# Sixteen expert blocks of the first ten tiles run while the last tiles are routed; weights split in 58 steps

## The chip, the cores and the metric
One core of one Trainium2 chip runs the whole program. The engines of the core are TensorE (PE), VectorE (DVE), ScalarE (ACT), GpSimd (POOL) and SyncE (SP), which mostly issues DMAs. The metric is the device time of one execution in microseconds; the median of the runs is compared.

## The reference
The input `x` is 2048 tokens (16 tiles of 128) of width 512. Four sublayers follow each other, each with a layer norm and a residual:
```
x = x + xattn0(layernorm(x), ctx, seg_id)       # 16 heads, keys masked to a window of 9 by seg_id
x = x + moe(layernorm(x))                       # 16 experts of width 352, 6 per token
x = x + xattn1(layernorm(x), ctx, mask)         # one head, 128 memory tokens
x = x + (mlp + product-key experts)(layernorm(x))
# moe:
scores = softmax(h @ gate_w.T); topk_w, topk_idx = top_k(scores, 6)
y = sum over e of cw[:, e] * ((silu(h @ w_gate[e].T) * (h @ w_up[e].T)) @ w_down[e].T)
```
All products are float32 in the reference; the kernel takes most of them as three float16 products (high times high, high times low, low times high).

## The kernel before, in words
The stretch of the program that matters runs from the first attention to the end of the mixture of experts.

**Attention (to about 576 us).** The loop runs over 64 steps (`STEPS`), four heads of one tile of 128 tokens in each. PE's step is `scores(m)`, the queries of the next tile (`heads_pe`, `rope_pe`), `turn_prob(m-2)`, `values(m-3)`, `outputs(m-4)`; ACT and DVE between them make exponentials, maxima and the high and low halves. When a tile's four steps are through, DVE adds its output to `x` (`add_outputs`) and the tile goes to routing some steps later: `token_rows` and `logits` on PE, softmax, the best six, a mask and a rank on DVE (`route_scores` ... `route_rank`). Tiles are routed in batches: two at a time, the last four one at a time. POOL's `place` writes, for each tile and each of its six choices, 128 token numbers of 4 bytes to the places in `expert_tokens` that the ranks give (96 indirect DMAs in all). ACT stores each tile's normalized row with its gate weights to `token_rows` (`row_store`) and `x` to `x_sum` (`x_store`).

**The split.** Beside it, `split_act` and `split_dve` turn the expert weights, in 128 pieces, into a high and a low half in `expert_w`: SP loads a piece into one of four stage buffers, ACT makes the high half (L1361), DVE the low one (L1578), SP stores both. Every step takes two pieces, so the split fills all 64 steps.

**The table.** When the last tile is ranked, PE counts tokens per expert (L1051 and before), DVE works out which block of 128 tokens belongs to which expert (L2005 to L2028) and writes a row of numbers (`tabrow`, L2031). Blocks are numbered 0 to 110 (`NBLK` = 111). SP waits for that row, for all stores to `token_rows` and for all places (L758 to L764), then loads the lists of the first blocks (`records`, L712 and L714) and the weights that are still missing.

**Experts (about 616 to 1300 us).** For block b POOL gathers 128 rows (`gather_rows`, L2298), PE turns them (`turn_rows`, L1061), does gate and up (`expert_up`, 24 matmuls), turns the hidden layer (`turn_hidden`, L1088) and does down (`expert_down`, 9 matmuls); ACT copies, takes silu and scales the result (`rows_out`), DVE multiplies and copies, POOL adds the result to `x_sum` by an indirect DMA with accumulation (L2311). Only one such add is in flight at a time. The blocks go in the order of the experts; four weight slots (`SLOTS`) are filled ahead, and `expert_loads` and `down_loads` refill a slot when its expert's last block is through. The weights of one expert are 1408 KB (`wa`) and 768 KB (`wd`).

After the last block the program reads `x_sum` back and goes on with the second attention and the MLP.

Each engine executes its own instructions in the order in which the program writes them; nothing reorders them. What decides is therefore where a call stands in an engine's list and which semaphore it waits for.

## Time and profile before
| | us |
|---|---|
| median of 3 runs | 1932.38 |
| lowest, highest | 1922.26, 1932.46 |
| the profiled execution | 1926.74 |
| its span | 1925.0 |
| TensorE busy in the span | 1801.6 |
| VectorE, ScalarE, GpSimd busy | 1093.7, 884.7, 820.2 |

The mean granted TensorE clock is 0.977 of full speed. Matmuls overlap, so a busy PE is one that always has a matmul under way. The stretches below are in microseconds from the start of the span: the head until about 96, attention until about 576, the experts from 616 to about 1300, the rest after that.

### The profile page before, as it was taken

The numbers are of one execution on the slowest core, as the hardware profiler recorded it, in microseconds if no ns is written. First come the engines' busy times: TensorE is split into PE (matmuls) and PEld (weight loads), VectorE is DVE, ScalarE is ACT, GpSimd is POOL, SyncE is SP. The second block draws the span as 40 slices with busy tenths as digits, with TensorE's granted clock in tenths as the row PEclk, the third lists the DMA queues.
The fourth block names the chain that finished last, engine by engine and source line by source line (L and its number), as shares of the span: only waits on it lengthen the run. The fifth ranks groups of instructions, "written<-read, shape, count | busy, mean of one in ns | idle before, by whom it ended". The sixth has DMA issues, their size and how long they took to land.

```text
span 1925.0 us, 39526 instructions
## 1 busy us (share of the span) xinstructions
PE 1801.6 (94%) x12786; PEld 1073.8 (56%) x12789; DVE 1093.7 (57%) x2985; ACT 884.7 (46%) x1833; POOL 820.2 (43%) x731
## 2 busy tenths in 40 slices
PE   6989999999972999999999999995899999999998
PEld 3566666766631666666666666663554444444444
DVE  4578888888852323322322323223656877777776
ACT  4588888888841443444434434433732221122111
POOL 4234456656664344443433443442112444544442
PEclk9999999999985999999999999998999999999999
DMA  8255587777776666766665765545012355555653
GB/s 310 88 163 175 178 164 168 186 178 170 182 161 166 159 147 145 160 163 152 146 150 135 165 153 100 93 82 129 33 35 66 125 187 202 206 171 210 203 178 143
DMA packets 137921, 294.81 MB, mean 153 GB/s; under 512 B 39200, under 2 KB 64416, under 8 KB 133600
## 3 DMA queue, kind: packets, MB, share of 16 engines
q1 hardware_dynamic: 86752, 157.47, 29.5%
q0 software_dynamic: 46368, 126.29, 26.7%
q10 hardware_dynamic: 4608, 8.52, 1.5%
q8 instruction: 115, 1.88, 0.4%
q14 instruction: 78, 0.64, 0.1%
HBM read 426.00 MB, written 78.33 MB: 262 GB/s over the span
## 4 chain that ended last, share of the span: by engine, by line
PE 81%; DVE 6%; DMA 4%; issue 4%; ACT 3%; POOL 1%; SPq 0%; another core or an unknown queue 0%; ACTq 0%; POOLq 0%; DVEq 0%
PE bank L234 21%; PE bank L236 21%; PE bank L235 21%; PE bank L1061 3%; PE bank L1088 2%; PE bank L851 1%; DVE work_arena L1578 1%; DMA x_sum<-x,work_arena 1%; PE bank L927 1%; ACT xt_arena L1314 1%; PE bank L842 1%; POOL expert_tokens L2226 1%; DMA work_arena<-in_ctxT 1%; DMA work_arena<-in_pk_w 1%; DMA work_arena<-in_moe_w 1%
## 5 line engine op out<-in xcount | busy, mean ns | idle before, releaser
L234 PE MATMUL bank<-work_arena,xt_arena 128*128 x1221 | 404.7, 331 | 2.8 <-DVE xt_arena L2072 1.9
L235 PE MATMUL bank<-work_arena,xt_arena 128*128 x1221 | 404.6, 331 | 0.0
L236 PE MATMUL bank<-work_arena,xt_arena 128*128 x1221 | 404.5, 331 | 0.0
L2311 POOL DMA_INDIRECT x_sum<-x,work_arena x111 | 176.5, 1590 | 392.5 <-DMA x_sum<-x,work_arena 222.9
L2060 DVE TENSOR_TENSOR xt_arena<-xt_arena,bank 128x352 f32<-128x352 f32 x111 | 57.9, 522 | 405.9 <-PE bank L236 373.0
L234 PE MATMUL bank<-work_arena 128*128 128x512 f16 (+1 forms) x600 | 226.3, 378 | 15.1 <-DVE x L1883 6.8
L235 PE MATMUL bank<-work_arena 128*128 128x512 f16 (+1 forms) x600 | 226.4, 379 | 0.0
L236 PE MATMUL bank<-work_arena 128*128 128x512 f16 (+1 forms) x600 | 226.3, 378 | 0.0
L1468 ACT ACTIVATE xt_arena<-bank 128x1024 f16<-128x1024 f16 x111 | 113.6, 1023 | 224.4 <-PE bank L1061 212.0
L234 PE MATMUL bank<-xt_arena,work_arena 128*128 128x512 f16 x528 | 200.1, 379 | 1.7 <-DVE xt_arena L194 1.7
L235 PE MATMUL bank<-xt_arena,work_arena 128*128 128x512 f16 x528 | 200.1, 379 | 0.0
L236 PE MATMUL bank<-xt_arena,work_arena 128*128 128x512 f16 x528 | 200.1, 379 | 0.0
L2318 POOL TENSOR_TENSOR work_arena<-work_arena 128x512 f16<-128x512 f32 x64 | 73.3, 1164 | 267.7 <-ACT work_arena L1453 267.7
L236 PEld LDWEIGHTS bank<-work_arena,xt_arena 128*128 128x128 f16 x1221 | 119.7, 98 | 85.1
L234 PEld LDWEIGHTS bank<-work_arena,xt_arena 128*128 128x128 f16 x1221 | 119.8, 98 | 82.6 <-issue 3.3
L235 PEld LDWEIGHTS bank<-work_arena,xt_arena 128*128 128x128 f16 x1221 | 119.7, 98 | 79.4
L2327 POOL DMA_INDIRECT work_arena<-in_pk_e,work_arena x128 | 135.0, 1055 | 36.7 <-issue 33.4
L2298 POOL DMA_INDIRECT x<-token_rows,work_arena x111 | 112.0, 1009 | 49.7 <-issue 27.7
L1578 DVE SCALAR_TENSOR_TENSOR work_arena<-work_arena 128x704 f16<-128x704 f32 (+2 forms) x90 | 89.9, 1001 | 70.8 <-ACT work_arena L1361 54.1
L2212 POOL TENSOR_TENSOR xt_arena<-xt_arena,work_arena 128x512 f32<-128x512 f32 x64 | 66.8, 1043 | 137.0 <-DVE work_arena L1668 133.9
L1314 ACT ACTIVATE xt_arena<-xt_arena,work_arena 128x128 f32<-128x128 f32 x256 | 123.2, 482 | 2.1
L1487 ACT ACTIVATE x<-bank,xt_arena 128x512 f32<-128x512 f32 x111 | 76.3, 687 | 99.6 <-PE bank L236 92.6
(278 smaller groups left out, 3823.0 us busy)
## 6 DMA issues: line engine op xcount, KB each, us to landing
work_arena<-expert_w SPq DMA_DIRECT2D x111, 1408.0 KB
work_arena<-expert_w SPq DMA_DIRECT2D x111, 768.0 KB
work_arena<-in_moe_w SPq DMA_DIRECT2D x64, 352.0 KB
expert_w<-work_arena SPq DMA_DIRECT2D x64, 352.0 KB
work_arena<-in_moe_w SPq DMA_DIRECT2D x64, 192.0 KB
expert_w<-xt_arena SPq DMA_DIRECT2D x64, 192.0 KB
work_arena<-in_mlp_w SPq DMA_DIRECT2D x8, 1536.0 KB
work_arena<-in_head_w SPq DMA_DIRECT2D x16, 512.0 KB, 5.6
```

The source lines that it names most:

```text
L234: pe.matmul(o, a_hi, b_hi, start=start, stop=False)
L235: pe.matmul(o, a_hi, b_lo, start=False, stop=False)
L236: return pe.matmul(o, a_lo, b_hi, start=False, stop=stop)
L1314: last = act.activation(prob[:, m % 3, i, :], prob[:, m % 3, i, :], ACT.Exp, bias=ebias[:, m % 4, i:i + 1], scale=seg_scale[:, t:t + 1], a ...
L1468: act.activation(xT[:, b % 2, :], bank[4][:, :].bitcast(F16), ACT.Copy).then_inc(xt_cp, 1)
L1487: act.activation(ysb[:, b % YB, :], bank[6 + b % 2][:, :], ACT.Copy, scale=ecw[:, b % 4, :]).then_inc(y_cp, 1)
L1578: return dve.scalar_tensor_tensor(out=o, in0=src, scalar=scale, in1=hi, op0=ALU.mult, op1=ALU.subtract)
L2212: pool.tensor_tensor(prob[:, m % 3, :, :], prob[:, m % 3, :, :], rinv[:, m % 4, :].unsqueeze(2).to_broadcast([P, 4, P]), ALU.mult).then_in ...
L2298: pool.indirect_dma_start(out=xbu[:, b % XB, :], out_offset=None, in_=rows[:, :], in_offset=bass.IndirectOffsetOnAxis(ap=rid[:, i:i + 1], ...
L2311: pool.indirect_dma_start(out=xacc[:, :], out_offset=bass.IndirectOffsetOnAxis(ap=rid[:, i:i + 1], axis=0), in_=ysb[:, b % YB, :], in_offs ...
L2318: pool.tensor_tensor(h_lo[:, S_ % 2, c, :], m2[:, c, :], h_hi[:, S_ % 2, c, :], ALU.subtract).then_inc(hlo, 1)
L2327: pool.indirect_dma_start(out=gbuf[:, n % 2 * SETS + i - FIRST[n], :], out_offset=None, in_=ins["pk_e"][:, :], in_offset=bass.IndirectOffs ...
```

## The change
A first part of the expert work is taken out of the tokens that are routed early. After ten tiles (`EARLY_TILES`) the tokens per expert are counted. Only whole blocks of 128 tokens of one expert count; the first 16 of them (`EARLY`) in the order of the experts become blocks 0 to 15, and the table for them is made on DVE in steps 61 and 62 (`early_blocks`, `early_columns`) and written after step 63 (`early_row`). SP takes the first four experts' numbers out of that table, and waits for the stores and places of the first ten tiles only. The other blocks follow as 16 to 110, with a table made while the early blocks run; the experts of the early blocks come up a second time in them, so that their weights are loaded twice. The last steps of routing move into the expert loop: tiles 14 and 15 (now one batch) are turned, ranked and counted between the matmuls of blocks 0 to 8, and 24 places move from before the first gather to behind it. `outputs(STEPS - 1)`, the last product of attention, comes after the first `turn_rows`. Banks are shared with the tail of attention, so that blocks below 13 (`EARLY_Y`) write their result to one bank instead of two. The attention arrays lie in another order in `work_arena`, and the tables lie elsewhere; the gate and up weights of three experts are loaded there before attention is over. The split of the 128 pieces is spread over the first 58 steps: 46 of them take two pieces and 12 take three, the last six take none.

The diff, cut to its core:
```diff
+SPLIT_STEPS = 58
+EARLY_TILES, EARLY = 10, 16
+EARLY_Y = 13
+assert (EARLY_TILES * P * TOPE - E * (P - 1)) // P >= EARLY
...
         att_a_lo = wr.take(H, 2 * P, dt=F16)
-        att_vo_hi = wr.take(H, D, dt=F16)
-        att_vo_lo = wr.take(H, D, dt=F16)
-        att_vo_end = wr.at
         PW, SW = DC * 384, 256 + 2048
...
+        att_vo_hi = wr.take(H, D, dt=F16)
+        att_vo_lo = wr.take(H, D, dt=F16)
+        att_vo_end = wr.at
...
-        BATCHES = [(a, 2) for a in range(0, NT - 4, 2)] + [(a, 1) for a in range(NT - 4, NT)]
-        INNER = len(BATCHES) - 2
+        BATCHES = [(a, 2) for a in range(0, NT - 4, 2)] + [(NT - 4, 1), (NT - 3, 1), (NT - 2, 2)]
+        INNER = len(BATCHES) - 1
...
+        EARLY_Q = next(q for q, (a, _) in enumerate(BATCHES) if a == EARLY_TILES)
+        COUNT_AT = ready(EARLY_Q) + 2
...
-            return [(i, i % NPC) for i in (2 * m, 2 * m + 1) if 0 <= i < E * NPC]
+            return [(i, i % NPC) for i in range(E * NPC) if i * SPLIT_STEPS // (E * NPC) == m]
...
+        def y_bank(b):
+            return bank[6] if b < EARLY_Y else bank[6 + b % 2]
...
+            def first_expert(r):
+                return sp.value_load(tabrow[0:1, FIRST_RUNS + r:FIRST_RUNS + r + 1], min_val=0, max_val=E - 1)
+            def first_a(r, e):
+                sp.dma_start(wa[:, r * 2 * AW:(r + 1) * 2 * AW],
+                             wsp[ds(e, 1), :, 0:2 * AW].rearrange("a p n -> p (a n)")).then_inc(load_a[r], 16)
+            def first_d(r, e):
+                at = (r + 1) % SLOTS * 2 * DW
+                sp.dma_start(wd[:, at:at + 2 * DW],
...
-            sp.wait_ge(routed, TABLE_ROW)
+            sp.wait_ge(q_free, q_at["early_cols",] + 1)
             sp.wait_ge(padded, 32)
-            sp.wait_ge(xacc_in, 16 * (NT + 1))
+            sp.wait_ge(xacc_early, 16 * (EARLY_TILES + 1))
             for s in range(SLOT_ROWS):
-                sp.wait_ge(row_out[s], 16 * len(range(s, NT, SLOT_ROWS)))
-            sp.wait_ge(placed, 16 * TOPE * NT)
-            sp.dma_start(rid[:, 0:1], recs[0:P, :]).then_inc(first_list, 16)
+                sp.wait_ge(row_out[s], 16 * len(range(s, EARLY_TILES, SLOT_ROWS)))
+            sp.wait_ge(placed_early, 16 * TOPE * EARLY_TILES)
+            firsts = [first_expert(r) for r in range(SLOTS)]
+            for s in range(STAGES):
+                sp.wait_ge(split_out[s], 16 * len(range(s, E * NPC, STAGES)))
+            sp.wait_ge(q_mm, q_at["heads", NT - 1, 3] + 1)
+            first_a(0, firsts[0])
             records(0)
-            records(1)
-            first_a(2)
-            first_d(3)
-            first_a(3)
+            first_a(1, firsts[1])
+            first_a(2, firsts[2])
+            sp.wait_ge(rope_h, 2 * NT)
+            sp.wait_ge(rope_l, 2 * NT)
+            sp.dma_start(rc2, ins["route_c2"]).then_inc(route_in, 16)
+            for n in range(1, EARLY // REC_BATCH):
+                records(n)
+            sp.wait_ge(y_mm, STEPS)
+            first_d(0, firsts[0])
+            first_a(3, firsts[3])
+            for r in range(1, SLOTS):
+                first_d(r, firsts[r])
             held = {}
             for b in range(NBLK + 5):
-                if b % REC_BATCH == 0 and 1 < b // REC_BATCH + 2 < (NBLK + REC_BATCH - 1) // REC_BATCH:
+                if b == MAIN_AT:
+                    sp.wait_ge(routed, TABLE_ROW)
+                    sp.wait_ge(xacc_in, 16 * (NT - EARLY_TILES))
+                    for s in range(SLOT_ROWS):
+                        sp.wait_ge(row_out[s], 16 * len(range(s, NT, SLOT_ROWS)))
...
+                if m == COUNT_AT:
+                    pe.wait_ge(masked, EARLY_Q + 1)
+                    q_room_free(pe, "early_count")
+                    pe.matmul(q_bank("early_count")[:, 0:E], one16, seen16, start=True, stop=True).then_inc(q_mm, 1)
...
+            pe.wait_ge(routed, EARLY_SET)
+            q_room_free(pe, "early_cols")
+            for i in range(4):
+                last = pe.matmul(q_bank("early_cols")[0:1, i * P:(i + 1) * P], tcol16[:, i:i + 1], id16[:, :],
+                                 start=True, stop=True)
...
+                if b == 0:
+                    pe.wait_ge(smax, STEPS)
+                if b == 1:
+                    pe.wait_ge(yadd, NT)
+                o = bank[1 if b == 0 else 4][:, :].bitcast(F16)
...
+                if 0 < b < EARLY_Y:
+                    pe.wait_ge(y_cp, b)
+                elif b >= EARLY_Y:
...
+            pe.wait_ge(q_free, q_at["early_cols",] + 1)
             slots = {b: slot_of(b) for b in range(2)}
             turn_rows(0)
+            outputs(STEPS - 1)
+            expert_up(0, slots[0])
             turn_rows(1)
-            expert_up(0, slots[0])
             for b in range(NBLK - 3):
                 expert_up(b + 1, slots[b + 1])
+                if b == 0:
+                    token_rows(14)
+                if b == 1:
+                    logits(14)
+                if b == EARLY_Y + 1:
+                    pe.wait_ge(routed, TABLE_ROW)
                 slots[b + 2] = slot_of(b + 2)
                 turn_rows(b + 2)
                 turn_hidden(b)
                 if b > 0:
                     expert_down(b - 1, slots.pop(b - 1))
+                if b == 1:
+                    pe.wait_ge(q_free, q_at["logits", 14] + 1)
+                    token_rows(15)
+                if b == 2:
+                    logits(15)
+                if b == 4:
+                    ranks(LASTQ)
+                if b == 5:
+                    route_count()
+                if b == 7:
+                    route_cols()
...
-            rows_turned(14)
             x_store(14)
             row_store(13)
             values_high(STEPS - 1)
-            gate_exps(Q14)
-            row_store(14)
-            row_high(15)
-            rows_turned(15)
-            x_store(15)
-            gate_exps(Q15)
-            row_store(15)
...
             rows_copy(0)
+            x_store(15)
+            row_high(15)
+            expert_silu(0)
             rows_copy(1)
-            expert_silu(0)
             hidden_high(0)
...
                 expert_silu(b + 1)
+                if b in (0, 2):
+                    rows_turned(14 + b // 2)
                 if b + 2 < NBLK:
                     rows_copy(b + 2)
                 hidden_high(b + 1)
+                if b == 2:
+                    gate_exps(LASTQ)
+                if b == 4:
+                    row_store(14)
+                    row_store(15)
             rows_out(NBLK - 2)
...
+            def early_blocks():
+                dve.wait_ge(rope_l, 2 * NT)
+                dve.wait_ge(q_free, q_at["early_count",] + 1)
+                dve.memset(run_up, 0.0)
+                dve.memset(early_sum, 0.0)
+                dve.memset(early_used, 0.0)
+                then(dve.tensor_tensor(tcmp, early_cnt.unsqueeze(2).to_broadcast([P, E, 15]),
+                                       rc_step.unsqueeze(1).to_broadcast([P, E, 15]), ALU.is_ge))
+                then(dve.tensor_reduce(early_full, tcmp, AX.X, ALU.add))
+                running_sum(early_end, early_full)
+                then(dve.tensor_scalar(early_sum[:, 1:E + 1], early_end, float(EARLY), None, ALU.min))
+                then(dve.tensor_tensor(early_used[:, 0:E], early_sum[:, 1:E + 1], early_sum[:, 0:E], ALU.subtract))
+                then(dve.tensor_scalar(early_is, early_used[:, 0:E], 0.0, None, ALU.is_gt))
+                running_sum(early_run, early_is)
...
+                if m == STEPS - 3:
+                    early_blocks()
+                if m == STEPS - 2:
+                    early_columns()
...
+            early_row()
...
+            add_outputs(15)
+            row_stats(15)
+            for s in range(STAGES):
+                dve.wait_ge(split_out[s], 16 * len(range(s, E * NPC, STAGES)))
+            dve.wait_ge(route_in, 16 * 8)
+            choose(0, EARLY, early_end, rc_blk[:, 0:EARLY])
+            row_normalize(15)
+            expert_weight(0)
             hidden(0)
             hidden_low(0)
             for b in range(NBLK):
-                expert_weight(b)
+                if b > 0:
+                    expert_weight(b)
                 if b == NBLK - 2:
                     hidden_copy(b)
                 if b + 1 < NBLK:
                     hidden(b + 1)
+                if b == 1:
+                    keep_logits(14)
                 if b != NBLK - 2:
                     hidden_copy(b)
                 if b + 1 < NBLK:
                     hidden_low(b + 1)
+                if b == 2:
+                    keep_logits(15)
+                    route_scores(LASTQ)
+                if b == 3:
+                    route_softmax(LASTQ)
+                    route_best(LASTQ)
+                    route_mask(LASTQ)
+                if b == 4:
+                    route_rank(LASTQ)
+                if b == 5:
+                    main_blocks()
+                    main_columns()
+                if b == 7:
+                    main_row()
+                if b == 8:
+                    choose(EARLY, NBLK, tend, rc_blk[:, 0:NBLK - EARLY])
                 if b in (20, 21, 23):
                     memory_masks((20, 21, 23).index(b))
...
-                if m in (STEPS - 2, STEPS - 1):
-                    place_batch(INNER - 2, 3 * (m - STEPS + 2), 3 * (m - STEPS + 3))
-            normalize(STEPS - 1)
-            row_rstd(14)
-            row_low(14)
-            place_batch(INNER - 1, 0, TOPE)
-            place_batch(Q14, 0, 1)
-            row_rstd(15)
-            row_low(15)
-            place_batch(Q14, 1, TOPE)
-            place_batch(Q15, 0, TOPE)
...
+            normalize(STEPS - 1)
+            row_rstd(14)
+            row_low(14)
+            gather_rows(0)
+            gather_rows(1)
+            gather_rows(2)
+            gather_rows(3)
+            row_rstd(15)
+            row_low(15)
+            gather_rows(4)
+            gather_rows(5)
+            gather_rows(6)
             for b in range(NBLK):
-                if b + ROWS_AHEAD < NBLK:
+                if b < 4:
+                    place_batch(INNER - 2 + b // 2, 3 * (b % 2), 3 * (b % 2) + 3)
+                elif b < 7:
+                    place_batch(LASTQ, 4 * (b - 4), 4 * (b - 3))
+                if ROWS_AHEAD + 2 <= b + ROWS_AHEAD < NBLK:
                     gather_rows(b + ROWS_AHEAD)
                 pool.wait_ge(y_cp, b + 1)
                 if b > 0:
```

On GpSimd's list the end of attention and the start of the experts read as follows before. `expert_tokens` is what `place` writes, `x<-token_rows` is a gather of rows, `x_sum<-x` the add of a block's result.
```order
L2222 TENSOR_TENSOR xt_arena<-xt_arena 128x512
L2226 DMA expert_tokens<-work_arena 38784x1 x3
L2212 TENSOR_TENSOR xt_arena<-xt_arena,work_arena 128x512
L2226 DMA expert_tokens<-work_arena 38784x1 x6
...
L2222 TENSOR_TENSOR xt_arena<-xt_arena 128x512
L2226 DMA expert_tokens<-work_arena 38784x1 x7
L2218 TENSOR_TENSOR ln_rs<-ln_ve,neg_half 128x1
L2222 TENSOR_TENSOR xt_arena<-xt_arena 128x512
L2226 DMA expert_tokens<-work_arena 38784x1 x11
L2298 DMA x<-token_rows,work_arena 128x528 x6
```
And now:
```order
L2416 TENSOR_TENSOR xt_arena<-xt_arena 128x512
L2476 DMA x<-token_rows,xt_arena 128x528 x4
L2412 TENSOR_TENSOR ln_rs<-ln_ve,neg_half 128x1
L2416 TENSOR_TENSOR xt_arena<-xt_arena 128x512
L2476 DMA x<-token_rows,xt_arena 128x528 x3
L2420 DMA expert_tokens<-work_arena 38784x1 x3
L2503 DMA x_sum<-x,xt_arena 2176x512
L2420 DMA expert_tokens<-work_arena 38784x1 x3
L2503 DMA x_sum<-x,xt_arena 2176x512
L2420 DMA expert_tokens<-work_arena 38784x1 x3
```
Seven gathers have moved ahead of the places of tiles 12 to 15, and those places stand between the adds of blocks 0 to 6, three or four at a time.

On SP's list the loads of the first experts before (`expert_w` 128x5632 is an expert's gate and up, 128x3072 its down, `expert_tokens` one block's list):
```order
L689 DMA work_arena<-in_route_c 128x367
L692 DMA work_arena<-expert_w 128x5632
L696 DMA work_arena<-expert_w 128x3072 x3
L692 DMA work_arena<-expert_w 128x5632
L765 DMA work_arena<-expert_tokens 128x1
L712 TENSOR_LOAD work_arena
```
And now, with a load of a number from the table (`TENSOR_LOAD`) ahead of each:
```order
L721 TENSOR_LOAD xt_arena
L721 ISA x2
L724 ISA
L724 DMA work_arena<-expert_w 128x5632
L739 TENSOR_LOAD xt_arena
L739 ISA x2
L741 ISA
L741 DMA xt_arena<-expert_tokens 128x1
...
L724 DMA work_arena<-expert_w 128x5632
L724 ISA
L724 DMA work_arena<-expert_w 128x5632
L803 DMA work_arena<-in_route_c 128x367
```
The first weight load now stands behind four numbers out of the table; the down weights come after twelve more lists and after the end of attention.

## Rows read from the trace of the kernel before

**Rows 1.** Page, forty slices: TensorE clock granted, in tenths.
```profile
PEclk9999999999985999999999999998999999999999
```

**Rows 2.** Windows: busy us by engine, PEclk, DMA share, GB/s.
```profile
96.00:480.00 384.00, 369.80 (x3825) 259.58 (x3824) 318.13 (x1027) 322.91 (x839) 206.38 (x183) 1.00 0.70 173
...
540.00:560.00 20.00, 13.83 (x89) 7.44 (x87) 11.08 (x43) 10.99 (x31) 16.02 (x16) 0.84 0.64 160
...
560.00:580.00 20.00, 13.60 (x80) 6.39 (x78) 9.39 (x36) 4.04 (x7) 8.61 (x9) 0.84 0.82 167
...
580.00:600.00 20.00, 2.45 (x27) 1.62 (x27) 6.79 (x37) 1.31 (x3) 11.91 (x12) 0.50 0.98 184
...
600.00:620.00 20.00, 5.21 (x28) 3.43 (x29) 3.48 (x5) 3.33 (x3) 6.44 (x5) 0.50 0.35 84
...
624.00:626.00 2.00, 2.00 (x18) 1.35 (x16) 0.38 (x3) 0.46 (x1) 0.00 (x0) 1.00 1.06 437
...
700.00:1300.00 600.00, 600.00 (x4480) 381.92 (x4479) 181.86 (x480) 243.07 (x380) 247.59 (x191) 1.00 0.63 136
```

**Rows 3.** Chain that ended last, 594 to 616: start, us, what.
```profile
594.89 11.17 DMA expert_tokens<-work_arena
...
610.12 1.97 DMA work_arena<-expert_tokens
...
612.35 3.15 DMA x<-token_rows,work_arena
```

**Rows 4.** Timeline of PE, 573 to 632: start, us, instruction.
```profile
573.38 0.38 PE L235 MATMUL bank<-work_arena 128*128 128x512 f16 x1
...
573.59 0.38 PE L236 MATMUL bank<-work_arena 128*128 128x512 f16 x1
...
615.82 1.01 PE L1061 MATMUL bank<-id,x 128*128 128x128 f16 x8 [1.21 <-DMA x<-token_rows,work_arena]
...
625.82 0.61 PE L1061 MATMUL bank<-id,x 128*128 128x128 f16 x8
...
631.22 0.61 PE L1061 MATMUL bank<-id,x 128*128 128x128 f16 x8
```

**Rows 5.** Timeline of SP's queue, 576 to 616.
```profile
576.27 0.34 SPq L692 DMA_DIRECT2D work_arena<-expert_w  x1
...
607.54 7.50 SPq L714 DMA_DIRECT2D work_arena<-expert_tokens  x7
```

**Rows 6.** Timeline of POOL, 562 to 643.
```profile
562.75 1.16 POOL L2222 TENSOR_TENSOR xt_arena<-xt_arena 128x512 f16<-128x512 f32 x1 [3.21 <-ACT xt_arena L1333]
...
593.62 0.97 POOL L2226 DMA_INDIRECT expert_tokens<-work_arena  x1 [0.30 <-issue]
...
635.11 1.63 POOL L2311 DMA_INDIRECT x_sum<-x,work_arena  x1 [14.16 <-ACT x L1487]
...
641.41 1.59 POOL L2311 DMA_INDIRECT x_sum<-x,work_arena  x1 [3.38 <-ACT x L1487]
```

**Rows 7.** Timeline of DVE, 547 to 592.
```profile
547.02 0.89 DVE L1578 SCALAR_TENSOR_TENSOR work_arena<-work_arena 128x704 f16<-128x704 f32 x1 [3.13 <-ACT work_arena L1361]
...
553.89 0.24 DVE L1714 TENSOR_TENSOR work_arena<-work_arena 128x16 f32<-128x16 f32 x1
...
588.06 0.41 DVE L2005 TENSOR_TENSOR work_arena<-bank,work_arena 128x240 f32<-128x240 f32 x1 [0.29 <-issue]
...
591.93 0.16 DVE L2028 SCALAR_TENSOR_TENSOR work_arena<-work_arena 128x1 f16<-128x1 f32 x1
```

**Rows 8.** Groups by form, 96 to 480: busy, mean ns, idle before.
```profile
L1361 ACT ACTIVATE work_arena<-work_arena 128x704 f16<-128x704 f32 x53 | 41.1, 775 | 0.9 <-DMA work_arena<-in_moe_w 0.9
...
L1361 ACT ACTIVATE xt_arena<-work_arena 128x384 f16<-128x384 f32 x53 | 27.0, 509 | 0.9 <-DMA work_arena<-in_moe_w 0.9
...
L1578 DVE SCALAR_TENSOR_TENSOR work_arena<-work_arena 128x704 f16<-128x704 f32 x53 | 47.3, 892 | 56.8 <-ACT work_arena L1361 43.5 <-issue 12.8
...
L1578 DVE SCALAR_TENSOR_TENSOR xt_arena<-work_arena,xt_arena 128x384 f16<-128x384 f32 x53 | 48.1, 907 | 0.0
```

307 lines of the change are left out of this document (179 added, 128 removed).

## The prediction
> **What bounds the kernel now.** I read the page's clock line first. The granted TensorE clock is full everywhere except in three of the forty slices of 48.1 us, the 12th and 13th (529 to 626 us) and the 28th (from 1299) [rows 1]. Then the windows. From 700 to 1300 PE is busy 600.00 of 600 us, from 96 to 480 it is 369.80 of 384: both long stages are bound by PE, with ACT at 322.91 and DVE at 318.13 of 384 close behind in attention [rows 2]. Between them lies the hole. From 540 to 620 PE is busy 13.83, 13.60, 2.45 and 5.21 of 20 us each, so 44.9 of 80 us are idle, and from 580 to 600 the granted clock is 0.50, the lower of the two levels (1.2 GHz) [rows 2].
>
> Then the chain of waits, to see what fills the hole. The last attention matmul starts at 573.59 [rows 4], SP sees its count at 576.27 [rows 5], and the first `turn_rows` that leads into `expert_up(0)` starts at 615.82 [rows 4]. In between stand the ranking of tiles 14 and 15, their places at 1.27 us each (0.97 busy and 0.30 issue) [rows 6], a landing of the last place of 11.17 us, the first list in 1.97 and the first gather in 3.15 us [rows 3]. None of it is PE's work. The change lets PE begin before it.
>
> **Where the blocks start afterwards.** I follow the new chain in the times of the old trace.
> DVE can write the early table when `route_scores` of step 63 is through, 553.89 + 0.24 [rows 7], since the two split pieces behind it are gone. Four small copies at about 0.2: 555.0.
> SP then loads four numbers, issues the first weights and loads four lists. Seven pairs of a number and a list take 7.50 us, 1.07 each [rows 5]; a DMA issue alone takes 0.34 of that [rows 5], a number 0.73. So 4 × 0.73 + 0.34 + 4 × 1.07 = 7.5: 562.5. The last list lands 1.97 later [rows 3]: 564.5.
> POOL is free by then: its `row_low(14)` stands at 562.75 [rows 6], and places that stood ahead of it are gone. Gather 0 lands after 3.15 [rows 3]: 567.7. It shares the DMA engines with 2.8 MB of weights that SP issues at 562.5; at 437 GB/s [rows 2] they take 6.6 us. Bounds: 567.7 if the gather slips between them, 574.3 if it comes behind all. I take 571, the middle, since there is no row of a gather under such load.
> PE gets there earlier: matmuls of 512 columns follow each other at 0.21 us (573.38, 573.59 [rows 4]), so an `outputs` of 12 takes 2.6, and `outputs(62)` ends that much before 573.97, at about 571.3; the split pieces gone from the last DVE and ACT lists give about 2 back. So PE waits 1 or 2 us for the gather, and `turn_rows(0)` is at 571.
> Then, at full clock: turn 0.5, `outputs(63)` 2.6, `expert_up(0)` 3.5 (24 matmuls of 352 columns, 24 × 0.21 × 352/512): 577.6. `turn_rows(1)` has its copy on ACT behind `row_high(15)` and `expert_silu(0)`, which wait for DVE's norm of tile 15: I put 3 us there. `expert_up(1)` 3.5, `token_rows(14)` 0.5: `turn_rows(2)` stands at 585.1, where it stands at 625.82 now [rows 4]. `turn_rows(3)`, with 1.6 for ACT's added copy, comes at 591.3 against 631.22 [rows 4]. The shift is 40 us. It includes the 3.5 us that `expert_up(0)` costs more now, at the lower clock of [rows 2].
>
> **What has to be paid back, term by term.**
> PE's small work for routing (two `token_rows`, two `logits`, rank, two tables) moves from an idle to a busy PE: about 1.5 us.
> POOL in blocks 2 to 6: three or four places at 1.27, a gather, taken like a place, at 1.27, and an add at 1.59 + 0.3 [rows 6] are 7.0 to 8.3 us, where one block takes 6.30 (641.41 − 635.11 [rows 6]). The lag is 2 × 0.7 + 3 × 2.0 = 7.4 us. Gathers are issued five blocks ahead and PE is up to two behind POOL, some 6 to 12 us of cover; so between 0 and 7. The places' own landing (11.17 once [rows 3]) can delay a gather behind them. I take 3, the bounds are 0 and 11.
> DVE's table work: 19 instructions from 588.06 to 592.09 [rows 7], 0.21 each. `main_blocks` and `main_columns` are 23, 4.9 us, in a block where DVE is busy 181.86/600 × 6.3 = 1.9 of 6.3 us [rows 2]: an overrun of 0.5, and PE needs that result only a block later. Nothing; without that cover 0.5.
> `early_blocks` and `early_columns` are 18 and 30 instructions, 3.8 and 6.4 us, in steps 61 and 62. There DVE waits now, 3.13 us at 547.02 for the split piece alone [rows 7], and two pieces (1.8 us) a step are gone. Net about 1 us later; the bounds are −3 (the pieces were the limit) and +6 (all of it on the path).
> The split over 58 steps: 12 steps with a third piece. ACT pays (41.1 + 27.0)/106 = 0.64 a piece, DVE (47.3 + 48.1)/106 = 0.90 [rows 8]. A step lasts 384/54 = 7.1 us (54 steps fit into these 384 us), ACT is busy 6.0 of it and DVE 5.9 [rows 2]; with a third piece 6.6 and 6.8. Still below 7.1, so PE sets the time: 1 us in all, with 0 and 12 × 0.9 = 11 as bounds.
> Weights: five experts (ten tiles give 480 tokens per expert on average, so mostly three whole blocks each) are loaded twice, 11 MB more, in a stage whose DMA share is 0.63 [rows 2]. The first four experts, 8.9 MB, must be in by block 3; at 437 GB/s that is 20 us, from 558 to 600 there are 42. Nothing; 0 to 5. One bank for the results: `expert_down(b)` waits for a copy that ACT does a whole `expert_up` earlier, nothing. The arena's order changes addresses only.
>
> Sum: 40 − 1.5 − 3 − 1 − 1 = 33.5 us. The profiled execution took 1926.74, which gives 1893. That is 5.6 below the median of the three runs and 4.5 above the lowest, so it stands for a middling run; I predict 1893.5.
>
> **A rule beside the rows.** The last place, 128 numbers of 4 bytes, took 11.17 us to land [rows 3]. The Trainium skill ("DMA: Bandwidth & Descriptors", section "Anatomy of one DMA — SWDGE (gpsimd) path") has about 2.0 us fixed plus the bytes at 436 GB/s for a DMA that GpSimd issues. For the place that is an estimate of 2 us, five times under the row; for a gather of 264 KB 2.6, and the row has 3.15 [rows 3]. By the page the POOL term would be 0 and the sum 36.5; I stay with 3, because the places here came in a dense series beside weight loads, and in the new order gathers stand among them. The same page ("Specifications") says that pieces under 512 bytes cost a read-modify-write, which speaks against putting 4-byte writes into the busy stage; the row does not separate that from queueing.
>
> **The rivals.**
> (a) The queue of small writes. Places, gathers and adds share POOL and one DMA queue; blocks 3 to 12 wait for their rows, because a gather stands behind four places and each add must have landed before the next. For it: the 11.17 us [rows 3] and 8.3 against 6.3 us. Against: the cover of two blocks. Price 10 to 15 more than my 3: about 1905. Chance 0.17.
> (b) Slower. The ring of four stage buffers sets the pace of attention: then the 58 steps take as long as the 64 do, the last six come on top with 6 × 7.1 = 43 us, and the 10.2 us of early tables are on the path too. 33.5 − 43 − 8 gives 17 slower, 1944. It decides from the point where a piece takes over 7.1/2.2 = 3.2 us round trip per stage. Against it: ACT waited only 0.9 us for 53 loads of each size [rows 8], and PE is busy 96% [rows 2]. Chance 0.04.
> (c) No gain: blocks start early, but PE stands at block 14 or before it for the second table, lists or weights until about the old time. SP's wait for the table needs DVE's last copy in block 7, two blocks before SP gets there; a slip of four blocks (25 us) leaves 8 us, 1919 to 1925. Chance 0.05.
> (d) Better. The last steps of attention, where PE is busy only 69% from 540 to 560 [rows 2], shrink by 6 us or so, and the places cost nothing: about 1884. Chance 0.16.
> My forecast, 1887 to 1900: 0.58.
>
> **How the numbers follow.** Half a percent, 9.7 us, is about what the runs can tell from no change. Faster by more: the forecast, (a), (d) and a part of (c), 0.91. Within: most of (c), 0.05. Slower: (b), 0.04. The range 1879 to 1912 takes in nearly all of (d) and of (a), with 1 to 2 in 10 left out.
>
> **What would show it.** In the new trace the first `turn_rows` starts near 571 and not after 575; the windows from 580 to 620 have PE busy at least 17 of 20 us and the clock at 1.00; `turn_rows(2)` is near 585. POOL's adds of blocks 2 to 6 are over 6.3 us apart and PE idles up to 3 us for rows around blocks 9 to 12; if it idles 10 or more, (a) holds. Attention's last matmuls before the table come at 551 ± 4; if at 590, (b). The end of the experts comes 30 to 37 us earlier than now. If attention is later by more than 10 us, or the blocks start after 590, the prediction is wrong.

## The result: slower by 1.3%

| | median of the runs | range |
|---|---|---|
| before | 1930.49 us | 1922.26 to 1932.46 |
| after | 1955.46 us | 1942.31 to 1961.43 |

The ratio is 1.0132, with 1.0079 to 1.0186 as its 95% interval. Measured once more beside other kernels it was 1.0100 [1.0072, 1.0127]. I had forecast 1893.5 us, a range of 1879 to 1912, and "slower" with 0.04. The prediction was wrong in sign.

The profiled execution of the changed kernel took 1942.31 us (span 1940.5), against 1926.74 (1925.0) before, 15.6 us more. It is the fastest of the four runs behind the second median, so the profiles account for 15.5 of the 25 us between the medians. The first sign is on the page: where [rows 1] have two low slices at the border of attention and experts, this line has three shallow ones.

```profile
PEclk9999999999998889999999999998999999999999
```

The windows, in the columns of [rows 2]:

```profile
96.00:480.00 384.00, 363.30 (x3739) 256.07 (x3737) 321.42 (x1015) 318.67 (x825) 207.79 (x177) 0.98 0.73 186
...
560.00:580.00 20.00, 15.78 (x91) 7.27 (x87) 12.59 (x60) 6.67 (x18) 5.82 (x6) 0.99 0.48 153
580.00:600.00 20.00, 10.46 (x63) 6.21 (x64) 4.38 (x12) 4.70 (x6) 7.30 (x8) 0.75 0.65 235
600.00:620.00 20.00, 15.69 (x135) 10.54 (x133) 3.82 (x12) 6.73 (x10) 6.07 (x6) 0.91 0.95 308
620.00:640.00 20.00, 19.12 (x154) 11.97 (x151) 7.30 (x31) 9.90 (x14) 12.59 (x12) 1.00 0.62 88
640.00:660.00 20.00, 15.15 (x95) 8.41 (x95) 8.81 (x43) 5.01 (x8) 7.58 (x8) 0.91 0.61 141
660.00:680.00 20.00, 14.58 (x93) 8.68 (x94) 4.73 (x12) 4.43 (x7) 14.48 (x13) 0.83 0.65 57
680.00:700.00 20.00, 12.14 (x76) 6.99 (x73) 5.92 (x15) 5.22 (x9) 6.46 (x5) 0.83 0.76 142
700.00:1300.00 600.00, 595.38 (x4420) 378.03 (x4421) 179.25 (x474) 240.66 (x377) 245.40 (x188) 0.99 0.66 154
```

The hole of [rows 2], with PE at 2.45 of 20 us, is filled in part: PE does 10.46 and 15.69 from 580 to 620. But from 640 to 700 it has only 41.87 of 60 us, at 0.83 to 0.91 of the clock. The DMA engines move 57 to 142 GB/s there at a busy share of 0.61 to 0.76. That pair alone says little: [rows 2] have 0.63 at 136 in the steady stage, where PE is full. The steady stage afterwards is as before, 595.38 of 600. What was won before 620 is lost again before 700, and more.

I followed two markers through each trace: the last maxima of an attention step (DVE), and the output of a block (ACT, `rows_out`), which comes every 6.3 us when nothing is in the way.

| marker, us | before | after | shift |
|---|---|---|---|
| maxima of step 24 | 268.2 | 276.0 | +7.8 |
| maxima of step 56 | 496.3 | 509.5 | +13.2 |
| maxima of step 63 | 547.9 | 563.0 | +15.1 |
| first `turn_rows` | 613.58 | 586.66 | −26.9 |
| output of block 0 | 634.1 | 615.8 | −18.3 |
| output of block 16 | 735.0 | 751.3 | +16.3 |
| end (span) | 1925.0 | 1940.5 | +15.5 |

The prediction calls the `turn_rows` at 615.82 the first that leads into `expert_up(0)`. It is that of block 1, which stood ahead of `expert_up(0)` in the old order. That of block 0 came before it:

```profile
613.58 1.03 PE L1061 MATMUL bank<-id,x 128*128 128x128 f16 x8 [20.97 <-DMA x<-token_rows,work_arena]
```

Blocks 0 to 16 take 34.6 us longer than sixteen periods; that is the largest piece. The chain of waits shows what stood there (start, us, what):

```profile
624.90 8.11 DMA x_sum<-x,xt_arena
...
633.77 16.67 DMA x_sum<-x,xt_arena
...
658.32 5.47 DMA x<-token_rows,xt_arena
...
675.75 8.95 DMA expert_tokens<-work_arena
...
694.79 9.58 DMA work_arena<-expert_w
```

Two adds took 8.11 and 16.67 us to land; before, the adds from 634 to 1300 have a median of 4.9 and a longest of 8.8. The last late place landed 8.95 us after 675.75. SP had waited for it, so the weights of block 10 came late; that is 7.4 of the 34.6 us, and the other 27.3 are lost up to block 9. POOL's timeline shows both ways in which a block gets longer there:

```profile
633.77 1.62 POOL L2503 DMA_INDIRECT x_sum<-x,xt_arena  x1 [2.05 <-DMA x_sum<-x,xt_arena]
...
651.20 1.61 POOL L2503 DMA_INDIRECT x_sum<-x,xt_arena  x1 [10.59 <-DMA x_sum<-x,xt_arena]
...
659.62 1.62 POOL L2503 DMA_INDIRECT x_sum<-x,xt_arena  x1 [0.30 <-issue]
```

From 651.20 to the next add are 8.42 us with no wait in them; this is POOL's own work: the add, four places and a gather. The 17.43 us ahead of it hold a wait of 10.59 for the landing of an add.

### The profile page after: what moved, and what is told of

The parts are those of the page before. It is cut to its first block, busy times and chain, and to the rows that moved or that the text cites. A ratio compares the mean times of both kernels' runs of the same rounds, so it can differ in the third digit from the quotient of the medians.

```text
span 1940.5 us, 39838 instructions
## 1 busy us (share of the span) xinstructions
PE 1814.2 (93%) x12789; PEld 1080.0 (56%) x12792; DVE 1105.8 (57%) x3038; ACT 885.8 (46%) x1834; POOL 829.6 (43%) x731
## 4 chain that ended last, share of the span: by engine, by line
PE 72%; DVE 8%; DMA 7%; issue 6%; ACT 4%; POOL 1%; SPq 1%; POOLq 0%; another core or an unknown queue 0%; ACTq 0%; DVEq 0%
PE bank L240 19%; PE bank L241 19%; PE bank L242 19%; PE bank L1118 2%; DMA x_sum<-x,xt_arena 2%; DVE work_arena L1660 2%; PE bank L1147 2%; PE bank L898 1%; ACT xt_arena L1393 1%; DVE xt_arena L1660 1%; DMA work_arena<-in_moe_w 1%; PE bank L974 1%; PE bank L889 1%; DMA x<-token_rows,xt_arena 1%; DVE xt_arena L1742 1%
## 5 line engine op out<-in xcount | busy, mean ns | idle before, releaser
L2503 POOL DMA_INDIRECT x_sum<-x,xt_arena x111 | 176.9, 1594 | 397.0 <-DMA x_sum<-x,xt_arena 223.0
L2476 POOL DMA_INDIRECT x<-token_rows,xt_arena x111 | 112.6, 1014 | 39.7 <-issue 28.8
L1560 ACT ACTIVATE x<-bank,work_arena 128x512 f32<-128x512 f32 x111 | 76.4, 688 | 107.6 <-PE bank L242 94.7
L2032 DVE SCALAR_TENSOR_TENSOR x<-bank,x 128x512 f32<-128x512 f32 x128 | 88.2, 691 | 59.2 <-PE bank L242 59.2
```

The source lines that it names most:

```text
L1560: act.activation(ysb[:, b % YB, :], y_bank(b)[:, :], ACT.Copy, scale=ecw[:, b % 4, :]).then_inc(y_cp, 1)
L2032: dve.scalar_tensor_tensor(out=xv, in0=bank[6 + q % 2][:, :], scalar=1 / (WS * WS), in1=xv, op0=ALU.mult, op1=ALU.add).then_inc(xadd[q % 2 ...
L2476: pool.indirect_dma_start(out=xbu[:, b % XB, :], out_offset=None, in_=rows[:, :], in_offset=bass.IndirectOffsetOnAxis(ap=rid[:, i:i + 1], ...
L2503: pool.indirect_dma_start(out=xacc[:, :], out_offset=bass.IndirectOffsetOnAxis(ap=rid[:, i:i + 1], axis=0), in_=ysb[:, b % YB, :], in_offs ...
```

## The experiments

Five groups of kernels ran, each with its own runs of the kernel before (medians 1920, 1936, 1926, 1923 and 1919 us). I compare ratios between groups and markers inside profiles. The ratios are those on record; the plain medians of the first group give somewhat others (0.9907 for a_noplace, 1.0113 for v1), and the groups ran on different chips. "Loss" is always the time of blocks 0 to 16 beyond sixteen periods.

### Group 1: the split, and the places taken away

**a_s64**: the changed kernel with the split over all steps.
```
-SPLIT_STEPS = 58
+SPLIT_STEPS = 64
```


> The changed kernel with the split over 64 steps again (two pieces in each), nothing else different. Theory 1 (the split over 58 steps costs attention 10 to 15 us: the third piece of a step waits for its load, 12.6 us of ACT's waits in the trace): step 63's maxima come within 4 us of where they come before (548), the total is 8 to 15 us under the changed kernel, 1940 to 1947. Rival A (attention is later because of the arena's order or the count): step 63 stays near 563 and the total at 1955. In both the loss in blocks 3 to 10 (35 us in the trace of the changed kernel) stays.

Measured: 1.0082 [1.0049, 1.0114]. Maxima of step 24 at 269.4 and of step 56 at 497.8, 1.2 and 1.5 us from the kernel before; of step 63 at 554.2. Loss 35.5. So the 58 steps cost time inside attention, the last three steps (24.4 us against 20.9 before) are late for another reason, and the loss in the blocks has nothing to do with either.

**b_s58**: the reverse, the kernel before with 58 steps.
```
-            return [(i, i % NPC) for i in (2 * m, 2 * m + 1) if 0 <= i < E * NPC]
+            return [(i, i % NPC) for i in range(E * NPC) if i * 58 // (E * NPC) == m]
...
```


> The kernel before with the split over 58 steps as the only edit. Theory 1: attention reaches step 58 some 10 to 15 us later, the last six steps give 2 to 5 back, total 5 to 12 us above before, 1936 to 1943. Rival A: total as before within 5 us.

Measured: 0.9998 [0.9977, 1.0020]. Step 56 is 6.2 us late, but the last six steps, free of split work, give it back: step 63 at 546.4. My expectation was wrong and its rival right.

**a_noplace**: the changed kernel without the 24 places of tiles 12 to 15; their tokens are missing from the lists and so from the experts' sum.
```
-                    sp.wait_ge(placed, 16 * TOPE * (NT - EARLY_TILES))
+                    sp.wait_ge(placed, 16 * TOPE * 2)
...
-                if b < 4:
-                    place_batch(INNER - 2 + b // 2, 3 * (b % 2), 3 * (b % 2) + 3)
-                elif b < 7:
-                    place_batch(LASTQ, 4 * (b - 4), 4 * (b - 3))
```


> The changed kernel without the 24 places of tiles 12 to 15: their tokens are missing from the lists, and pad rows stand in for them, so the number of gathers, adds and matmuls is the same. Theory 2 (the places stand in one DMA queue ahead of each add, which then lands after 8 to 17 us instead of 5, and PE runs out of rows and of result buffers): the blocks keep a period of 6.3 us from block 1 on, the loss of 35 us in blocks 3 to 10 is gone, total 1918 to 1928. Rival B (the loss comes from double loads of expert weights or from the routing work on DVE and PE): the loss stays at 20 us or more, total above 1940.

Measured: 0.9883 [0.9851, 0.9916], 22 us faster than before (17.9 by the medians). Loss 2.4 where the changed kernel loses 34.6. Its windows (columns as above) are what I had forecast for all of the stage:

```profile
620.00:640.00 20.00, 20.00 (x152) 12.54 (x150) 12.27 (x60) 8.30 (x14) 7.04 (x6) 1.00 0.80 228
640.00:660.00 20.00, 20.00 (x150) 12.53 (x149) 9.85 (x24) 7.97 (x13) 8.76 (x7) 1.00 0.62 128
660.00:680.00 20.00, 18.95 (x142) 11.90 (x141) 5.58 (x15) 7.54 (x13) 7.96 (x6) 1.00 0.97 298
```

PE is nearly full and its clock is whole, with everything else of the change in place but SP's wait for the places. The missing tokens change what the blocks hold, not their number. That pad rows land sooner is not what helps: the adds of blocks 0 to 16 land in 5.2 us (median), against 4.9 in the kernel before.

**v1**: the 12 places of tiles 12 and 13 among the first seven gathers, the 12 of tiles 14 and 15 three at a time in blocks 4 to 7.
```
+            place_batch(INNER - 2, 0, TOPE)
+            place_batch(INNER - 1, 0, 1)
             row_rstd(15)
...
+            place_batch(INNER - 1, 1, TOPE)
             for b in range(NBLK):
-                if b < 4:
...
+                if 4 <= b < 8:
+                    place_batch(LASTQ, 3 * (b - 4), 3 * (b - 3))
```


> The changed kernel with 12 of the 24 late places (tiles 12 and 13) issued before the first add, in GpSimd's idle time around the first seven gathers, and the other 12 three at a time in blocks 4 to 7. Theory 2: adds of blocks 0 to 3 land in about 5 us, the loss in the blocks falls from 35 to 10 to 18 us, total 1932 to 1942. If the number of places and not their order against the adds decides, the loss stays above 28 us and the total at 1950 or more.

Measured: 1.0071 [1.0039, 1.0103], loss 39.6. The sum hides two things. Up to block 8 this kernel loses 15.5 us and the changed kernel 27.0, so with half of the places between adds half of that part goes. But the last place now stands ahead of the add of block 7 and lands 8.60 us after 672.78, SP waits for it, and output 9 comes 24.9 us after output 8, with PE waiting for weights (total, times, longest):

```profile
PE bank L240 <- DMA work_arena<-expert_w: 20.6, 3, 14.5
```

Blocks 9 and 10, with late weights, lose 24.2 of the 39.6 us here.

### Group 2: which places, and whose wait

**b_late24**: the kernel before with 24 places more, into a tensor of their own. SP waits for them only after the last block.
```
...
+                if b < 4:
+                    for k in range(3 * (b % 2), 3 * (b % 2) + 3):
+                        place_again(12 + b // 2, k)
+                elif b < 7:
+                    for k in range(4 * (b - 4), 4 * (b - 3)):
+                        place_again(14 + k // TOPE, k % TOPE)
```


> The kernel before, with 24 more small writes: the entries of tiles 12 to 15 are written once more, into a list tensor of their own that nothing reads, three before each of the adds of blocks 0 to 3 and four before each of blocks 4 to 6, where the changed kernel has its own. Nothing else changes, attention above all. Theory (the writes stand in one DMA queue with the adds and the gathers and slow these): blocks 0 to 16 lose 25 to 40 us and the time is 20 to 35 us above the kernel before, 1940 to 1955. Rival (the loss of the changed kernel comes from what else it does in these blocks: routing the last two tiles, the wait of SP for the writes, first weights late): under 8 us.

Measured: 1.0101 [1.0081, 1.0121], loss 28.8 where there was none. This is the cleanest proof: attention, tables and weights are those of before, and the writes alone bring the loss. (The profiled run is the slowest of its four; by the medians the kernel is 21.4 us slower.) POOL's timeline (start, us, line, operation, and in brackets how long POOL stood before it and for what):

```profile
671.55 1.59 POOL L2325 DMA_INDIRECT x_sum<-x,work_arena  x1 [2.56 <-DMA x_sum<-x,work_arena]
673.45 1.01 POOL L2305 DMA_INDIRECT expert_again<-work_arena  x1 [0.30 <-issue]
...
678.93 0.99 POOL L2300 DMA_INDIRECT x<-token_rows,work_arena  x1 [0.31 <-issue]
686.58 1.60 POOL L2325 DMA_INDIRECT x_sum<-x,work_arena  x1 [6.66 <-DMA x_sum<-x,work_arena]
```

From one add to the next are 15.0 us. Issuing four places and a gather ends at 679.92; then POOL still stands 6.66 us for the add of 671.55 to land. So of the 8.7 us over the period POOL's own time is about 2 and the landing the rest.

**c_sp**: the changed kernel, with SP's wait for the late places behind that turn's weight loads.
```
-                if b == MAIN_AT:
-                    sp.wait_ge(routed, TABLE_ROW)
...
                     down_loads(b - 5, held.pop(b - 5))
+                if b == MAIN_AT:
+                    sp.wait_ge(routed, TABLE_ROW)
...
```


> The changed kernel, with SP's wait for the last 24 writes (at block 10 of its loop) standing behind that turn's weight loads instead of ahead of them. If the wait's cost is that the weights of block 11 are issued late, the interval of about 13 us around blocks 9 to 11 goes and 4 to 8 us with it, 1932 to 1938 on this chip beside 1940 for the changed kernel. If the queue of adds sets the pace whatever SP does, under 3 us.

Measured: 1.0150 [1.0117, 1.0182], no faster than the changed kernel's 1.0132. Loss 30.5 instead of 34.6 (31.7 when the changed kernel ran again), with 6.9 us lost later. The edit did not do what it was made for: the interval at block 10 is 12.22 us where it was 13.67, and PE still waits 4.4 us for weights there (4.9 before the edit), since the weights of SP's next turn stand behind the wait. So c_sp does not separate late weights from slow adds.

**v1_nolast**: as v1, without the 12 places of tiles 14 and 15 (their tokens are missing).
```
-                    sp.wait_ge(placed, 16 * TOPE * (NT - EARLY_TILES))
+                    sp.wait_ge(placed, 16 * TOPE * 4)
...
-                if 4 <= b < 8:
-                    place_batch(LASTQ, 3 * (b - 4), 3 * (b - 3))
```


> The changed kernel with the 12 writes of tiles 12 and 13 ahead of and among the first seven gathers (as in the version with reordered writes), and without the 12 writes of tiles 14 and 15, so that only 12 of the 24 late writes are made, and none between the adds. If the price is about the same for each write, wherever it stands, blocks 0 to 16 lose about half of the changed kernel's 35 us, 15 to 20, and the time is 1915 to 1922. If only the writes that stand between adds cost, the loss is under 8 us and the time that of the version without any of them, about 1902 to 1908.

Measured: 1.0035 [1.0006, 1.0065], loss 2.8. The 12 places before the first add cost 0.4 us in the blocks (2.8 against 2.4 with no late place at all). From block 0's output on only those between adds cost. The time stayed above before. Attention in this group's changed kernels ended at 569 to 579 (b_late24, beside them: 557). And from the last maxima to block 0's output it took 59.9 us here, 49.1 in a_noplace. The other kernels with these places among the first gathers show the same (v2 60.1, v3 59.7, v3s 66.6) except v1 (51.8); the changed kernel and c_start, without them, take 52.8 and 49.0. Whether the early places have a part in this is not shown.

**v2**: 20 early blocks, the places of tiles 12 and 13 as in v1, the last 12 two at a time in blocks 5 to 10, SP's wait behind the loads.
```
-EARLY_TILES, EARLY = 10, 16
+EARLY_TILES, EARLY = 10, 20
...
+                if 5 <= b < 11:
+                    place_batch(LASTQ, 2 * (b - 5), 2 * (b - 4))
```


> The changed kernel with 20 early blocks instead of 16, the 12 writes of tiles 12 and 13 ahead of and among the first gathers, the 12 of tiles 14 and 15 two at a time before the adds of blocks 5 to 10, and SP's wait for them behind that turn's weight loads (block 14). If what costs is how many writes stand ahead of one add (three or four), two at a time cost little: loss over blocks 0 to 16 under 15 us, 1915 to 1922. If each write costs its share wherever it stands in the block stage, the loss stays near 20 us and the time at 1922 to 1932.

Measured: 1.0177 [1.0151, 1.0203], loss 31.4, and 11.2 more later. Twelve places, two at a time, cost as much as 24 had, and PE does not wait for weights here.

### Group 3: one go, fewer numbers, tables twice

**v3s** and **v3**: the places of tiles 12 and 13 as in v1, all 12 of tiles 14 and 15 in one go before the add of block 5, SP's wait behind the loads, with 64 and 58 split steps.
```
+                if b == 5:
+                    place_batch(LASTQ, 0, 2 * TOPE)
```


> The changed kernel with the split over all 64 steps, the 12 writes of tiles 12 and 13 ahead of and among the first gathers, all 12 writes of tiles 14 and 15 in one go behind the gather of block 10 and before the add of block 5, and SP's wait for them behind that turn's weight loads. If each change between writes and adds costs its own delay, one long stretch of writes costs once, some 16 us of issues less what three output buffers hide: loss over blocks 0 to 16 of 8 to 15 us instead of 30 to 40, and the time 0.985 to 0.998 of the kernel before. If each write costs about 2.5 us wherever it stands among the adds, the loss stays at 25 to 35 and the time at 1.005 to 1.015.

> The same kernel as the one with all 12 writes in one go, with the split over 58 steps as in the changed kernel, so that the pair shows what the 58 steps are worth there. From the runs so far (the changed kernel with 64 steps ended attention 5 to 9 us earlier than with 58), I expect it 3 to 8 us slower than its twin with 64 steps. If the split over 58 steps helps, it is faster than its twin.

Measured: 1.0074 [1.0045, 1.0103] and 1.0072 [1.0049, 1.0095]. Losses 19.6 and 21.0: of the ways tried, one go loses least, but it is not cheap. The twins are equal: with 64 steps the last maxima are 8.0 us sooner (554.5, 562.5), but the first `turn_rows` only 1.1 (585.2, 586.3), because SP issues the first weights at 565.82 and 569.05: with 64 steps its last split stores, at 559.39 and 559.86, and the store of a tile of `x` stand ahead of them.

**b_p16**: b_late24 with 16 tokens in each place instead of 128.
```
-out_offset=bass.IndirectOffsetOnAxis(ap=ridx[:, t, k:k + 1], axis=0),
+out_offset=bass.IndirectOffsetOnAxis(ap=ridx[0:16, t, k:k + 1], axis=0),
...
```


> The kernel before with the 24 more writes in the first seven blocks, each of them for 16 tokens only instead of 128. If the price of a write is in its 128 entries (descriptors and their four-byte stores), the loss over blocks 0 to 16 falls from 29 us to under 8 and the time to within 0.4% of the kernel before. If it is a price per DMA (issue, order in the queue, its completion), the loss stays over 20 us.

Measured: 1.0116 [1.0097, 1.0135], loss 20.6. An eighth of the numbers keeps the time (1.0101 with 128 numbers, on another chip) and 72% of the loss (28.8). Most of the price is per DMA.

**c_twice**: the changed kernel with `early_blocks` and `early_columns` done twice.
```
...
                     early_blocks()
+                    early_blocks()
...
+                    early_columns(False)
                     early_columns()
```


> The changed kernel with the vector engine's work for the early tables (steps 61 and 62, 4.4 and 5.3 us in the trace) done twice. If this work lies open at the end of attention, the last three steps take 9 to 10 us more than the changed kernel's 23.4 and the first rows go out that much later; the time is 7 to 10 us (0.4 to 0.5%) above the changed kernel's. If it is hidden beside the steps, under 3 us.

Measured: 1.0146 [1.0127, 1.0166]. The last three steps (maxima of 60 to maxima of 63) take 31.1 us, against 23.4 in the changed kernel and 16.4 in b_s58, which has no tables there. So the tables lie open: 7.0 us more than in b_s58 once, 7.7 more when doubled. The kernel before, with split pieces in these steps, takes 20.9. DVE's timeline in the changed kernel shows them, first and last of each table:

```profile
551.03 0.39 DVE L1875 TENSOR_TENSOR work_arena<-xt_arena,work_arena 128x240 f32<-128x240 f32 x1
...
555.21 0.18 DVE L1866 TENSOR_TENSOR work_arena<-work_arena 128x16 f32<-128x16 f32 x1
...
557.59 0.23 DVE L1898 TENSOR_SCALAR work_arena<-work_arena 128x16 f32<-128x16 f32 x1
...
562.82 0.16 DVE L1917 SCALAR_TENSOR_TENSOR work_arena<-work_arena 128x1 f16<-128x1 f32 x1
```

4.4 and 5.4 us in a row, with the next step's maxima right behind them and no idle time of DVE between.

### Group 4: the start, and the routing put first

**v4** and **v4s** (58 and 64 steps): attention's last outputs before block 0 on PE, tiles 14 and 15 routed beside blocks 0 and 1, all 24 late places before the first add, first lists and first down weights earlier on SP, its wait for the places behind the loads. Of the edit only the end of GpSimd's part is shown.
```
...
+            place_batch(INNER - 1, 0, TOPE)
+            gather_rows(5)
+            gather_rows(6)
+            place_batch(LASTQ, 0, 2 * TOPE)
             for b in range(NBLK):
```


> The changed kernel with the last two tiles routed at once: attention's last outputs ahead of the first block on the matrix engine, the routing of tiles 14 and 15 beside blocks 0 and 1 instead of 1 to 5, all 24 late writes before the add of block 0 and none between adds; SP fetches the first lists before the first weights, the first down weights before the other lists, and waits for the writes behind the weight loads. Theory (writes cost only between adds; the start was late by the order of issues): blocks 0 to 16 lose under 10 us, block 0's output comes at 600 to 612, and the time is 0.985 to 0.998 of the kernel before. Rival (routing now stands in the way of blocks 0 to 2, and what it holds up there is as much as the writes cost later): 1.000 to 1.010.

> The same kernel with the split over all 64 steps. The pair with one go of writes showed no difference in time (1.0072 and 1.0074), attention 8 us shorter but the first block no sooner. Here the first lists are fetched before the weights and wait for nothing of the split but its end; if the end of the split holds them, it is 0 to 3 us slower than its twin, and if attention's end decides, 3 to 8 us faster.

Measured: 1.0077 [1.0052, 1.0102] and 1.0056 [1.0028, 1.0085], losses 25.2 and 22.6. The times lie where the rival put them. POOL in v4s:

```profile
602.05 0.97 POOL L2475 DMA_INDIRECT x<-token_rows,xt_arena  x1 [0.30 <-issue]
613.76 1.02 POOL L2419 DMA_INDIRECT expert_tokens<-work_arena  x1 [10.74 <-DVE work_arena L1838]
...
629.27 1.60 POOL L2501 DMA_INDIRECT x_sum<-x,xt_arena  x1 [0.31 <-issue]
639.97 1.59 POOL L2501 DMA_INDIRECT x_sum<-x,xt_arena  x1 [9.10 <-DMA x_sum<-x,xt_arena]
```

The places come at 613.76, when DVE has ranked, and block 0's output (614.2) then waits until 629.27 for its add; that add takes about 10 us. POOL needs 15.5 us to issue the 12 places, and ahead of the first add nothing covers that. v4s has the lowest ratio of the variants that compute everything, but its interval overlaps those of v1, v3, v3s, v4, a_s64 and of the changed kernel's second measurement; all are above 1.

**c_start**: the changed kernel with only the orders on SP and of `outputs(63)` on PE changed.
```
-            turn_rows(0)
             outputs(STEPS - 1)
+            turn_rows(0)
...
+            records(0)
             first_a(0, firsts[0])
-            records(0)
...
```


> The changed kernel with two orders alone changed: SP fetches the first lists before the first weights and the first down weights before the other twelve lists, and the matrix engine does attention's last outputs ahead of turn_rows(0). If these orders made the start late, block 0's output comes 5 to 12 us sooner after attention's last maxima than the changed kernel's 53 us, but the queue of adds still loses 30 to 35 us in blocks 0 to 16; the time falls by what the start gains, 5 to 12 us below the changed kernel's on this chip. If the landing of the gathers under the weights' traffic decides, under 3 us.

Measured: 1.0095 [1.0067, 1.0122] beside 1.0100 for the changed kernel. From the last maxima to block 0's output 49.0 instead of 53.3 us; loss 32.5, and 12.0 later. The start was earlier by 4, and nothing of it reached the end.

**a_again**: the changed kernel.

> The changed kernel itself, on the same chip and in the same rounds as the three beside it. From the ratio of the first measurement, 1.0132 with 1.0079 to 1.0186, both theories expect 1.008 to 1.019 again; blocks 0 to 16 lose 30 to 38 us and attention's last maxima stand 10 to 16 us later than in the kernel before.

Measured: 1.0100 [1.0072, 1.0127], loss 31.7, last maxima at 561.2.

### Group 5: one place at a time

**b_one24**: the kernel before, one place more in each of the blocks 8 to 31.
```
...
+                if 8 <= b < 32:
+                    place_again(12 + (b - 8) // TOPE, (b - 8) % TOPE)
```


> The kernel before, with the 24 additional writes one by one: one ahead of each of the adds of blocks 8 to 31, far from the start. If what costs is several writes ahead of one add, the 1.2 us that an add has to spare in each 6.3 us period and the two output buffers hide a single one: rows come out at 6.3 us all through and the time is within 0.2% of before. If each write delays its add by about 1.7 us net (41 us for 24, of which the buffers hid 12, in the version with three and four), 24 of them cost 25 to 30 us again less what each period spares: 5 to 20 us.

Measured: 1.0176 [1.0136, 1.0216]. Blocks 0 to 16 lose 6.1 and the later ones 21.9, 28.0 in all, more than either expectation; the first late output is that of block 12, four blocks after the first write, when the three buffers are used up. Three intervals of 11.2 to 12.9 us, at blocks 21, 28 and 33, make 18 of the 28.0. The DMA issues from 684 to 840 (engine, operation, count, median us to landing), of this kernel:

```profile
x<-token_rows,work_arena POOLq DMA_INDIRECT x22, 6.2
x_sum<-x,work_arena POOLq DMA_INDIRECT x21, 6.6
```

and of the kernel before:

```profile
x_sum<-x,work_arena POOLq DMA_INDIRECT x25, 5.0
```

And POOL's adds, of b_one24 and then of before:

```profile
690.22 1.59 POOL L2321 DMA_INDIRECT x_sum<-x,work_arena  x1 [4.43 <-DMA x_sum<-x,work_arena]
692.12 1.02 POOL L2305 DMA_INDIRECT expert_again<-work_arena  x1 [0.30 <-issue]
693.44 0.99 POOL L2300 DMA_INDIRECT x<-token_rows,work_arena  x1 [0.30 <-issue]
699.23 1.59 POOL L2321 DMA_INDIRECT x_sum<-x,work_arena  x1 [4.80 <-DMA x_sum<-x,work_arena]
```

```profile
686.68 1.58 POOL L2311 DMA_INDIRECT x_sum<-x,work_arena  x1 [2.61 <-DMA x_sum<-x,work_arena]
...
692.74 1.58 POOL L2311 DMA_INDIRECT x_sum<-x,work_arena  x1 [3.19 <-DMA x_sum<-x,work_arena]
```

Each add waits for the landing of the one before, since both may touch the same row of the sum. Here the pair is 6.06 us apart without a place, where a block takes 6.3. Single intervals without a place lie between 5.5 and 9.5 us, so one pair proves little. But over the 106 adds from 634 to 1300 the landing takes 5.33 us on average, and the next add is issued 0.77 after it: 6.10, so the chain of adds has about 0.2 us to spare. A single place raises the median landing by 1.6 us. An estimate from these medians is 24 × (1.6 − 0.2) = 34 us, less the cover of the buffers, against 28.0 measured. Spreading the places thinly, one per block, does not help.

**b_s58_again**: b_s58 on other runs.

> The kernel before with the split over 58 steps once more, on another chip or rounds. If the 58 steps alone make the split's loads late, the maxima of step 24 stand 3 us or more later than the 268.2 of the kernel before (as in the changed kernel's profiles); if it is 58 steps together with what else the changed kernel does there, they stand within 2 us of it and the time is within 0.3% of before, as in the first run.

Measured: 1.0012 [0.9995, 1.0029]. Step 24 at 271.2 (3.0 late), step 56 at 503.1, step 63 at 547.0.

## Why the prediction was wrong, by its own steps

**The POOL term, sized 3 us within 0 and 11, was 32.** This step failed and decided the sign. The mechanism is that of rival (a): it had the right queue and the right waits ("each add must have landed before the next"), but a price of 10 to 15 more; it was 29 more. Loss 34.6 with the late places and 2.4 without gives 32.2. Of this some 7 us came through SP, which waited for the last place and then loaded weights late. That is the wait of rival (c), at block 10. I had counted POOL's issue time (7.0 to 8.3 us per block), and took it for what a block costs. The count itself was right: the two intervals without a wait, ahead of the adds of 659.62 and 678.35, are 8.42 and 8.47 us. The landing was left out. [rows 6] show adds 6.30 us apart, and I read the period as set by PE alone. POOL's wait for the landing of its adds stood in the trace of before, from 684 to 840 this line (total, times, longest), and I did not ask how much that chain has to spare:

```profile
POOL x_sum L2311 <- DMA x_sum<-x,work_arena: 79.0, 23, 6.6
```

It has about 0.2 us a block. What a place between adds lengthens a landing by is then paid nearly in full once the three buffers are used up. The cover of two blocks that I held against it exists for the gathers, which are issued five blocks ahead, and not for the adds. POOL's waits from 600 to 700 in the changed kernel (total, times, longest) show it:

```profile
POOL x_sum L2503 <- DMA x_sum<-x,xt_arena: 24.3, 4, 10.6
```

The total is no sign by itself (a_noplace has 25.6 us in six such waits and loses nothing); the longest wait is, 10.6 against 6.0 us.

PE waited for rows too, 16.3 us in five waits from 600 to 720, so gathers behind places and held-up adds are late as rival (a) said.

**The price of a place by its bytes.** One place of 128 numbers per block lengthens an add by 1.6 us (medians), and the last late place landed after 8.95. The Trainium skill ("DMA: Bandwidth & Descriptors", "Anatomy of one DMA — SWDGE (gpsimd) path") has about 2.0 us plus the bytes at 436 GB/s for a DMA that GpSimd issues, which makes an estimate of 2.0 us for a place. The runs disagree: the place took 8.95 us, and the POOL term was not 0 but 32. With 16 numbers instead of 128, 72% of the loss stayed (20.6 of 28.8 us). The Trainium skill says on the same page ("Specifications") that under 512 bytes a DMA engine does a read-modify-write. Such a price would go by the pieces, and in b_p16 most of the loss did not.

**The tables in steps 61 and 62, sized 1 us net within −3 and +6, were 2.5 net.** The last three steps take 20.9 us before and 23.4 in the changed kernel, so the term was within its bounds. Its working was not right. Without split work these steps take 16.4 us (b_s58): the pieces that go give 4.5 back and the tables cost 7.0. I had set the tables against waits of 3.13 us [rows 7], but these waits were for the split pieces, which were gone. Removing the cause of a wait removes the cover too.

**The split over 58 steps, sized 1 us within 0 and 11.** In b_s58 step 56 comes 6.2 and 6.8 us late and the end 0.9 to 1.5 early. With the rest of the change, pairs of 58 and 64 steps on the same chip differ at step 63 by 1.9 and 4.8 us (v1 and a_noplace against a_s64), 8.0 (v3) and 3.0 (v4): more than 1, and within the bounds. But in the profiled run step 56 came 13.2 late, beyond the bound of 11, and step 63 15.1 late. My own sign for a wrong prediction, attention later by more than 10 us, was met. There is one gap of 12.6 us between the maxima of steps 22 and 23 where [rows 8] has no such wait. ACT's waits from 96 to 560 in the changed kernel:

```profile
ACT work_arena L1441 <- DMA work_arena<-in_moe_w: 12.6, 5, 6.4
```

and in b_s58_again:

```profile
ACT work_arena L1361 <- DMA work_arena<-in_moe_w: 11.0, 5, 4.0
```

So rival (b)'s ring does set the pace at a few steps, for a few microseconds and not for 43. With 64 steps the same waits are 2.8 us in all (a_s64). Over all profiles with 58 steps, the changed kernel and its variants reach step 56 at 503.7 to 526.7, b_s58 at 502.5 and 503.1; with 64 the variants reach it at 497.8 to 499.3. Part of that spread is the chip: b_late24, which leaves attention as it was, reaches it at 504.4 on the chip of the latest ones. Why 58 steps cost the changed kernel more than the kernel before stays open; the other order of the arena was not tried by itself.

**The start of the blocks, forecast 571, was 586.66.** From 580 to 620 PE is busy 10.46 and 15.69 of 20 us at a clock of 0.75 and 0.91, where I had asked for 17 at 1.00. The table's row on DVE came at 565.50 instead of 555.0: 10.5 of the 15.7 us are attention. SP takes 9.0 us to the issue of the fourth list (7.5 forecast), and the landings take 3 more than I gave them. SP and PE of the changed kernel:

```profile
569.31 0.37 SPq L724 DMA_DIRECT2D work_arena<-expert_w  x1
...
577.51 17.46 SPq L741 DMA_DIRECT2D xt_arena<-expert_tokens  x12
595.16 0.35 SPq L729 DMA_DIRECT2D work_arena<-expert_w  x1
```

```profile
586.66 1.03 PE L1118 MATMUL bank<-id,x 128*128 128x128 f16 x8 [9.52 <-DMA x<-token_rows,xt_arena]
...
594.88 0.61 PE L1118 MATMUL bank<-id,x 128*128 128x128 f16 x8
...
602.40 0.61 PE L1118 MATMUL bank<-id,x 128*128 128x128 f16 x8
...
607.65 0.47 PE L240 MATMUL bank<-work_arena,xt_arena 128*128 x1 [4.31 <-ACT xt_arena L1540]
```

The last list landed in 3.79 us and the gather in 7.67, where [rows 3] have 1.97 and 3.15. Those two are not of block 0, though: 3.15 is the gather of block 1; that of block 0 was issued at 608.50 and its `turn_rows` began at 613.58. The 7.67 lie between my bounds for the gather, 3.15 and 9.75. `turn_rows(2)` at 602.40 is 23.4 us sooner than 625.82 [rows 4], not 40. From the first `turn_rows` to block 0's output it takes 29.1 us where it took 20.6: PE waits 7.2 us for ACT's copies (4.6 forecast), which stand behind `row_high(15)` and `rows_turned(14)`, and the first matmuls after the 9.52 us wait take 0.43 each instead of 0.22, at the lower clock level (the window's mean is 0.75).

**PE's small routing work, 1.5,** and main tables and weights, 0: a_noplace keeps all of them and loses 2.4 in the blocks. Both within what I gave them. SP's wait for the late places, which I had only inside rival (c), stood at block 10 and not 14. The late weights behind it go with 7.4 us in the changed kernel and 24.2 in v1. That wait ends with the landing of the last place, so it is a second way in which the places cost time; b_late24 loses 28.8 us without it.

The sum with measured terms, in the profiled pair: block 0's output 18.3 sooner, blocks 0 to 16 34.6 later: 16.3 slower, and the spans differ by 15.5. Without late places the same change is 18 to 22 us faster than before (a_noplace); so of the 33.5 us a half to two thirds were there, and the places turned them round.

## What to carry to other kernels

Before work is moved into a stage that looks bound by one engine, look for the second chain in it, its period and what it has to spare: here adds that wait for one another's landing run at about 6.1 us beside a PE at 6.30. Work of another kind put into that chain's queue lengthens the landings. Here 12 or 24 places among the adds cost 15 to 31 us in every order tried (15.5 in v1 up to block 8, 31.4 in v2), and 24 of them one by one over 24 blocks cost 28. And what waits for such work elsewhere, here SP with the next weights, pays once more. A wait that serves as cover for added work is cover only if its cause stays.

## What the runs showed of the hardware

- A small indirect write costs its neighbours in GpSimd's DMA queue: adds land in 6.6 instead of 5.0 us (medians) with one place per block. With three or four places around them single adds took 14 to 17 us (16.67 in the changed kernel, some 14 in b_late24), where the longest before is 8.8. With 16 numbers per place instead of 128 the time was the same (1.0116, 1.0101), and the loss 20.6 instead of 28.8 us.
- The same writes cost the blocks nothing when no add follows closely: 12 places among the first gathers changed the loss from 2.4 to 2.8 us. The start before it was slower in four of the five kernels that have them, for a cause that is not shown.
- The DMA engines' busy share and rate do not tell whether a queue is held up: from 640 to 660 the changed kernel has 0.61 at 141 GB/s with PE at 15.15 of 20 us, a_noplace 0.62 at 128 with PE at 20.00.
- Seven variants of the changed kernel (c_sp, v2, v3, v3s, v4, v4s, c_start) lost 7 to 12 us more in single gaps after block 16, where the kernel before, the changed kernel and b_late24 lose under 1. They are the seven that order SP's loads otherwise; the other variants lose 0.6 to 5.7. PE waits for gathers in these gaps; in c_start the one into the longest (12.3 us) took 10.16 to land. Why SP's order has this effect stays open.
